# Eight x tiles in flight, LoRA loads in one place, first mixing blocks issued by ScalarE, and weighted factors rounded ahead of the second layer's rows

## The reference, cut to what matters

```python
# layer 0: per sequence, rows mixed by a 64x64 matrix
y = einsum('bct,bcd->bdt', x, L0_cond_weights[itok_B_0_15])
h = relu(layernorm(y @ gw1.T + gb1) * gamma + beta)        # 32 hidden units
gates = h @ gw2.T + gb2                                    # 8 experts, the best 2, softmax
w = factors of the two experts, 0 where an expert has over 768 tokens
x1 = x + y @ weight.T + einsum((y @ lora_A) * w, lora_B) / 16   # 8 experts x rank 16
# layer 1: per sequence one of 8 weights of 1024x1024
z = einsum('bsi,boi->bso', x1, L1_cond_weight[itok_B_3_7])
gate, up = bitlinear(z, w_gate), bitlinear(z, w_up)        # weights rounded to -1, 0, 1 by mean |w|
out = x1 + bitlinear(gate * up, w_down)
```

## Time and profile before

| | us |
|---|---|
| median of 3 executions | 1399.43 |
| lowest, highest | 1396.98, 1400.17 |
| the profiled execution's own time | 1401.02 |
| its span, first to last instruction | 1399.3 |
| TensorE busy | 1330.5 (95% of the span) |
| VectorE, ScalarE, GpSimd busy | 726.4, 391.1, 157.4 |
| mean granted TensorE clock | 0.985 |

### The profile page before, as it was taken

The page is one execution under the profiler, slowest core; times in us unless marked ns, Lnnn a source line. Parts: engine busy times, 40 slices in busy tenths (PEclk is TensorE's granted clock), DMA queues, the critical chain, the costliest instruction groups (busy, mean ns, idle before and its releaser), DMA issues.

```text
span 1399.3 us, 24300 instructions
## 1 busy us (share of the span) xinstructions
PE 1330.5 (95%) x8864; PEld 850.5 (61%) x8865; DVE 726.4 (52%) x1143; ACT 391.1 (28%) x437; POOL 157.4 (11%) x114
## 2 busy tenths in 40 slices
PE   6787699999999998999999999999999999999998
PEld 5773344444454444555544788854788844888843
DVE  5375455411255565888865355573355582455521
ACT  3464343200111135888730011120011110111100
POOL 5100000000101000000000023320133310222310
PEclk9998899999999999999999999999999999999999
DMA  9976699967996926999964643353634455544354
GB/s 235 231 255 212 249 401 416 346 166 149 284 264 227 272 98 241 354 361 350 315 251 159 237 150 136 143 216 128 222 150 157 147 188 186 205 157 153 128 196 143
DMA packets 174626, 310.70 MB, mean 222 GB/s; under 512 B 99392, under 2 KB 131520, under 8 KB 166752
## 3 DMA queue, kind: packets, MB, share of 16 engines
q1 hardware_dynamic: 156048, 242.77, 53.6%
q10 hardware_dynamic: 14032, 43.97, 8.8%
q0 software_dynamic: 4480, 23.07, 4.6%
HBM read 220.78 MB, written 68.03 MB: 206 GB/s over the span
## 4 chain that ended last, share of the span: by engine, by line
PE 79%; DMA 8%; DVE 4%; issue 3%; ACT 2%; SPq 2%; POOL 1%; ACTq 0%; DVEq 0%; POOLq 0%
PE pair L969 27%; PE pair L1006 15%; PE pair L841 12%; PE pair L933 10%; PE pair L757 9%; DMA region_w<-in_L_ffn_w_gate 2%; DMA region_q<-wb_scratch 2%; PE pair L668 2%; PE pair L887 2%; DMA w1s_scratch<-region_q 1%; PE pair L764 1%; ACT region_w L1088 1%; POOL region_w L653 1%; SPq L448 1%; ACT region_q L1039 1%
## 5 line engine op out<-in xcount | busy, mean ns | idle before, releaser
L969 PE MATMUL pair<-act_t,region_q 128*128 128x256 f16 x3696 | 404.0, 273 | 0.0
L969 PEld LDWEIGHTS pair<-act_t,region_q 128*128 128x128 f16 x3696 | 361.6, 98 | 42.5
L1006 PE MATMUL pair<-region_q,region_w 128*128 128x512 f16 x1232 | 267.6, 379 | 4.7 <-DMA region_q<-wb_scratch 4.4
L1006 PEld LDWEIGHTS pair<-region_q,region_w 128*128 128x128 f16 x1232 | 120.1, 98 | 150.9 <-DMA region_q<-wb_scratch 5.9
L653 POOL TENSOR_TENSOR region_w<-region_q,region_w 128x1792 f32 (+1 forms) x33 | 118.4, 3588 | 732.4 <-ACT region_w L1244 732.4
L841 PE MATMUL pair<-region_w,act_t 128*128 x816 | 180.2, 381 | 2.0 <-DVE region_q L1571 2.0
L757 PE MATMUL pair<-region_w,act_t 128*128 128x512 f16 x768 | 172.5, 382 | 0.0
L933 PE MATMUL pair<-act_t,region_q 128*128 128x512 f16 x704 | 157.9, 383 | 1.4 <-issue 1.4
L841 PEld LDWEIGHTS pair<-region_w,act_t 128*128 x816 | 80.2, 98 | 95.8 <-issue 4.3
L1250 ACT ACTIVATE region_q<-pair 128x512 f32<-128x512 f32 x33 | 19.7, 597 | 403.7 <-PE pair L969 403.7
L757 PEld LDWEIGHTS pair<-region_w,act_t 128*128 (+1 forms) x768 | 75.6, 99 | 88.2 <-issue 2.5
(11 more groups left out here) (184 smaller groups left out, 1016.4 us busy)
## 6 DMA issues: line engine op xcount, KB each, us to landing
region_q<-wa_scratch SPq DMA_DIRECT2D x33, 1792.0 KB, 7.3
region_q<-wb_scratch SPq DMA_DIRECT2D x28, 1408.0 KB, 5.9
region_q<-in_L_cond_weight SPq DMA_DIRECT2D x40, 512.0 KB, 9.4
w1s_scratch<-region_q ACTq DMA_DIRECT2D x40, 512.0 KB, 7.9
wa_scratch<-region_q SPq DMA_DIRECT2D x22, 896.0 KB, 6.2
region_q<-in_x SPq DMA_DIRECT2D x64, 256.0 KB, 6.5
region_w<-in_L_ffn_w_gate ACTq DMA_DIRECT2D x17, 640.0 KB, 5.4
wb_scratch<-region_q SPq DMA_DIRECT2D x11, 896.0 KB, 4.1
```

Source lines behind the costliest of these rows:

```text
L969: mm = pe.matmul(bank(s_bank, b)[:, (1 - h) * HALF:(2 - h) * HALF], ring_a[s][:, h, o_a, k], moving[a], start=(opens and h == 1 and k == 0 ...
L1006: mm = pe.matmul(bank(s_bank, b), iop[:, a, p, o_a, tp * P:(tp + 1) * P], ring_b[r][:, p], start=(opens and p == 0 and a == 0), stop=(not ...
```

## The change

- x goes through eight buffers (`NMIX`), a tile at a time, SP reading eight fields of the order at once; the buffer of tile t is free when tile t-8 is mixed. All LoRA-A loads stand ahead of tile 8, LoRA B behind tile 15.
- The mixing blocks of tiles 0 and 1 are issued by ScalarE, before its first rounding; GpSimd starts with tile 2.
- Gate products start after the mix of tile 9; LoRA A is rounded after tile 8; w_gate loads start at tile 10; square roots are taken at tiles 12 and 14, and that of the third quarter behind the loop, where its moments are now taken too. In the moments the mean's scaling and the subtraction are one instruction.
- Blocks 4 to 7 of the first adapter are rounded and stored behind the weighted factors, between the first x1 parts, on ScalarE and on VectorE.
- SP loads tiles 2 and 3 of x together and then the eight row blocks of the second adapter.
- The second layer's first product waits for 15 residuals.

```diff
@@ -71,8 +71,10 @@
 SUMS = {11: (0,), 12: (1, 2), 13: (3, 4), 14: (5, 6), 15: (7, 8)}
-GATES = {11: (0, 1), 12: (2, 3, 4), 13: (5, 6, 7), 14: (8, 9, 10, 11), 15: (12, 13, 14, 15)}
-LORA_AFTER = {2: (1,), 4: (2, 3), 6: (4, 5), 8: (6, 7)}
+GATES = {9: (0, 1), 10: (2, 3), 11: (4, 5), 12: (6, 7), 13: (8, 9, 10), 14: (11, 12), 15: (13, 14, 15)}
+NMIX = 8
+SQRTS = {12: 0, 14: 1}
+LORA_AT = 8
 NPIECE = 24
@@ -129,7 +131,7 @@
         x1_nat = [view(region_q, 40 + 4 * i, [D], F32) for i in range(2)]
-        mix_nat = [x_nat[0], x_nat[1], view(region_q, 48, [D], F32), view(region_q, 52, [D], F32)]
+        mix_nat = [view(region_q, kb, [D], F32) for kb in (32, 36, 48, 52, 16, 20, 24, 28)]
         gw1_nat = x1_nat[0]
@@ -441,12 +444,11 @@
             def load_mix(t, perm):
-                for s in range(2):
-                    wait_if(sp, y_done, t + s - 3)
-                    slot = (t + s) % 4
-                    for h in range(2):
-                        sp.dma_start(mix_nat[slot][h * SEQ:(h + 1) * SEQ, :], x_rows[ds(perm[2 * s + h] * SEQ, SEQ), :])\
-                          .then_inc(mix_loaded[slot], 16)
+                slot = t % NMIX
+                wait_if(sp, y_done, t - NMIX + 1)
+                for h in range(2):
+                    sp.dma_start(mix_nat[slot][h * SEQ:(h + 1) * SEQ, :], x_rows[ds(perm[h] * SEQ, SEQ), :])\
+                      .then_inc(mix_loaded[slot], 16)
@@ -455,17 +457,18 @@
                 load_w(w0[r * P:(r + 1) * P, :], r, r)
-            load_lora(0)
             sp.wait_ge(index_ready, 1)
-            for t in range(0, NT, 2):
-                load_mix(t, fields(sp, F_PERM + 2 * t, 4, NB - 1))
-                if t < 4:
-                    for r in range(4 + t, 6 + t):
-                        load_w(w0[r * P:(r + 1) * P, :], r, r % 4)
-                for k in LORA_AFTER.get(t, ()):
-                    load_lora(k)
-                if t == 10:
-                    sp.dma_start(lora_b_nat, lora_b.rearrange("e r o -> (e r) o")).then_inc(lora_b_loaded, 16)
+            for t0 in range(0, NT, 4):
+                perm = fields(sp, F_PERM + 2 * t0, 8, NB - 1)
+                for t in range(t0, t0 + 4):
+                    if t == LORA_AT:
+                        for k in range(KC):
+                            load_lora(k)
+                    load_mix(t, perm[2 * (t - t0):2 * (t - t0) + 2])
+                    if t in (1, 4):
+                        for r in range(4, 6) if t == 1 else range(6, 8):
+                            load_w(w0[r * P:(r + 1) * P, :], r, r % 4)
+            sp.dma_start(lora_b_nat, lora_b.rearrange("e r o -> (e r) o")).then_inc(lora_b_loaded, 16)
             sp.wait_ge(index_ready, INDEX_ALL)
@@ -497,7 +500,16 @@
-            with sp.Fori(1, 6) as i:
+            for t in range(2, 4):
+                sp.wait_ge(acc_released, t - 1)
+                load_pair(x_nat[t - 2], x_loaded[t - 2], t)
+            used = field(sp, F_USED, 0, NADP)
+            row_1 = field(sp, F_ADP, 1, NADP - 1) * D
+            with sp.If(used > 1):
+                for t in range(2, 4):
+                    for q in range(4):
+                        load_w(w1_rows[ds(row_1 + (4 * t - 8 + q) * P, P), :], NPREP0 + 4 * t + q, q)
+            with sp.Fori(2, 6) as i:
                 layer0(i)
@@ -611,7 +623,7 @@
                 for s in range(2):
-                    wait_if(pool, cond_loaded[c + s], 32 * i)
+                    wait_if(pool, cond_loaded[c + s], 32 * i if c > 0 else 0)
                     for h in range(2):
@@ -619,7 +631,7 @@
             for i in range(2):
-                for c in range(0, 8, 2):
+                for c in range(2 - 2 * i, 8, 2):
                     load_cond(i, c)
@@ -711,7 +723,7 @@
                 pe.wait_ge(mix_loaded[slot], loads)
-                pe.wait_ge(cond_loaded[t % 8], 32 * (t // 8 + 1))
+                pe.wait_ge(cond_first[t] if t < 2 else cond_loaded[t % 8], 32 * (t // 8 + 1 if t % 8 > 1 else 1))
                 wait_if(pe, y_low, t - 1)
@@ -735,7 +747,7 @@
                     pe.wait_ge(index_ready, INDEX_ALL)
-                mix(t, t % 4, (t + 1) % 2, 32 * (t // 4 + 1))
+                mix(t, t % NMIX, (t + 1) % 2, 32 * (t // NMIX + 1))
                 if t == 0:
@@ -829,7 +841,7 @@
                     pe.wait_ge(x1_low, 2)
-                    pe.wait_ge(acc_released, NT)
+                    pe.wait_ge(acc_released, NT - 1)
                 pe.wait_ge(w1_loaded, rank * 16 + 16)
@@ -1044,6 +1056,13 @@
+            act.wait_ge(index_ready, 1)
+            act.wait_ge(consts_ready, 8)
+            cond = fields(act, F_COND, 4, 15)
+            for t in range(2):
+                for h in range(2):
+                    act.dma_start(cond_bd[h * SEQ:(h + 1) * SEQ, t, h * SEQ:(h + 1) * SEQ],
+                                  cond_rows[ds(cond[2 * t + h] * SEQ, SEQ), :]).then_inc(cond_first[t], 16)
             high_w0(0)
@@ -1094,8 +1113,6 @@
                     tmp_part(n)
-                if t == 13:
-                    gate_sqrt(0)
                 y_part(t, (t + 1) % 2)
@@ -1104,20 +1121,22 @@
                     act.dma_start(small[t - 2][0], small[t - 2][1].partition_broadcast(P)).then_inc(small_loaded, 16)
-                if t in (9, 10):
-                    load_gate(t - 9)
                 if t == 10:
+                    for p in range(2):
+                        load_gate(p)
+                if t == 8:
                     act.wait_ge(lora_loaded, 16 * KC)
...
                         .then_inc(ag_high, 1)
-                if t >= 14:
-                    gate_sqrt(t - 13)
+                if t in SQRTS:
+                    gate_sqrt(SQRTS[t])
                 for p in SUMS.get(t, ()):
...
             high(lb[:, 0, :], lora_b_nat, WGT_SCALE).then_inc(ag_high, 1)
+            gate_sqrt(2)
@@ -1132,16 +1151,12 @@
                 store_w(o, o)
-                rank0_part(o + 4)
-                sum_gate(13 + o)
-            sum_gate(17)
-            for o in range(4, 7):
-                store_w(o, o - 4)
+            for p in range(13, 17):
+                sum_gate(p)
             for i in range(2):
...
                 high(tmpw_t[:, 0, i * D:(i + 1) * D], pair[2][:, :], 1.0).then_inc(tmpw_high, 1)
-                if i == 0:
-                    store_w(7, 3)
+            sum_gate(17)
@@ -1157,8 +1172,16 @@
+            rank0_part(4)
+            rank0_part(5)
+            store_w(4, 0)
             x1_part(0, 0)
+            rank0_part(6)
+            store_w(5, 1)
             x1_part(1, 1)
+            rank0_part(7)
+            store_w(6, 2)
+            store_w(7, 3)
             with act.Fori(1, NT // 2) as i:
@@ -1467,8 +1490,8 @@
                 gthen(v.tensor_reduce(tot, hq, X, ALU.add))
-                gthen(v.tensor_scalar(tot, tot, 1.0 / GH, None, ALU.mult))
-                gthen(v.tensor_tensor(hq, hq, per_tile(tot, GH), ALU.subtract))
+                gthen(v.scalar_tensor_tensor(out=hq, in0=per_tile(tot, GH), scalar=-1.0 / GH, in1=hq,
+                                             op0=ALU.mult, op1=ALU.add))
                 gthen(v.tensor_tensor(sq, hq, hq, ALU.mult))
@@ -1500,19 +1523,20 @@
                     low_w0(t + 3)
-                if t == 10:
+                if t == 8:
                     v.wait_ge(ag_high, 2)
...
                         ag[:, 0, :, 0:ER]).then_inc(ag_low, 1)
-                if t == 12:
+                if t == 11:
                     v.wait_ge(small_loaded, 80)
                     gate_moments(0)
+                elif t == 12:
                     gate_logits(0)
...
                     gate_logits(1)
-                    gate_moments(2)
+            gate_moments(2)
             gate_logits(2)
@@ -1556,8 +1580,6 @@
             ins.then_inc(tmpw_ready, 1)
-            for o in range(4, KC):
-                low_w(o, o - 4)
             for i in range(2):
@@ -1584,9 +1606,13 @@
             residual(1, 1, pair[1])
+            low_w(4, 0)
+            low_w(5, 1)
             low_x1(0)
             residual(2, 0, pair[3])
+            low_w(6, 2)
             low_x1(1)
+            low_w(7, 3)
             prep_low(1, 2)
```

More of the change, by code:

```diff
@@ L230, in build_program @@
         w_loaded = [sem(f"w_loaded{i}") for i in range(4)]
-        mix_loaded = [sem(f"mix_loaded{i}") for i in range(4)]
+        mix_loaded = [sem(f"mix_loaded{i}") for i in range(NMIX)]
         cond_loaded = [sem(f"cond_loaded{i}") for i in range(8)]
+        cond_first = [sem(f"cond_first{i}") for i in range(2)]
         x_loaded = [sem(f"x_loaded{i}") for i in range(2)]
```

## The result

| | before | after |
|---|---|---|
| median (lowest to highest, executions) | 1399.18 (1396.98 to 1401.44, 8) | 1393.07 (1387.89 to 1396.11, 8) |
| ratio, 95% interval | | 0.9953 [0.9935, 0.9971] |
| profiled execution, its span | 1401.02, 1399.3 | 1387.89, 1386.2 |

The change makes the kernel 6.1 us faster, where 21 were forecast; 1393 lies outside the range of 1367 to 1391. The profiled execution is the fastest of the eight. It won 8.7 us up to the second layer's first product (330.1 to 321.4); the other 4.4 of its 13.1 lie behind that product, where the changed stages play no part: from there to the end it took 1064.8 us, and 1069.2 before. As far as the runs show this is chance: in the 18 profiles of this document that rest ranges from 1064.8 to 1069.5 us, and in a second one of the changed kernel (after_again) it was 1068.9.

The account below looks back on a forecast made before the run. It took TensorE's waits before 177.5 us, then a DMA-bound adapter stage, as the bound; 5.5 (opening) + 13.4 (adapter stage) + 2.0 (last residual) = 20.9 off gave 1378 us, 8 in 10 within 1367 to 1391.

Parts of the forecast that it names:

- the larger term (stores behind the factors): First adapter's rounds and stores behind the factors: next adapter stage starts earlier, worth 13.4 us (8 to 17).
- the opening: Eight tiles, LoRA loads together, first blocks by ScalarE: start of first main product (E) 5.5 us earlier (0 to 9).
- 42 to 50, I take 46: Opening: tile 8 of x arrives at 46 us, first gate product near 52, first main product (E) at 92.
- The late root: Gate chain: third quarter's root behind copies and LoRA B's round ends the factors' multiply about 4 us later; 1 shows.
- Rival A: Opening gives nothing, as eight tiles share saturated DMA engines and E stays; 1384 us, chance 0.15.
- Its wait of 17.9 becomes 1.0 + 3.8 = 4.8: TensorE's wait for the rounded factors, once stores no longer precede them: 4.8 us (2 to 10).
- Rival D: Factors stay blocked: gate pieces 15 and 16 take 12.31 us, factors 6 us later; 1384 us, chance 0.12.
- 3.9 us behind the residual: with the change E+47.7: Next adapter's first row load follows the second residual by 3.9 us, at E+47.7 instead of E+63.1: 15.4 earlier.
- So this is a DMA chain: First row load to TensorE's turn of tile 10, 107.3 us, is DMA-bound; 15.4 earlier less 2 for stores gives 13.4.
- my test of 113 us: Forecast is wrong if first row load to TensorE's turn of tile 10 takes over 113 us.
- The last residual, 2.0: Second layer's first product no longer waits for the last tile's residual: 2.0 us earlier (0 to 2.0).
- Rival B: Adapter stage gets dearer as loads, stores and blocks 4 to 7 mix; 1443 us at 260 GB/s, chance 0.07.

Follow-up runs that it names:

- lora_flat: Changed kernel with LoRA A's bytes read by one load of 128 long rows instead of eight loads of small packets; 1388.94 us.
- late_root: Kernel before with only the third quarter's square root moved behind the last gate copies and LoRA B's round; 1403.89 us, ratio 1.0024.
- opening_root_early: Kernel before with only the opening part, third quarter's root ahead of the last gate copies, gate sums 8 and 9 later; 1401.23 us, ratio 1.0006.
- sums_behind: Changed kernel with gate sums 15 and 16 behind the factors' rounds and 17 behind the last store; 1384.39 us.
- rows_as_before: Changed kernel with SP's old order of x tiles 2 and 3 and the next adapter's row blocks; 1393.61 us.
- three: Changed kernel with the square root early, the gate sums behind the factors and the old row order together; 1381.67 us, ratio 0.9870.
- half_rows: Changed kernel with row loads of the second to fifth adapters cut to 512 of 1024 columns; 1391.25 us.
- factors_only: Kernel before with only the rounds and stores of weight blocks 4 to 7 moved behind the weighted factors; 1393.37 us.
- three_flat: Changed kernel with root early, sums behind, old row order, and LoRA A's bytes in 128 large packets; 1375.42 us.
- all_residuals: Changed kernel with the second layer's first product waiting for all 16 residuals again; 1394.42 us.

## Why the prediction was wrong, step by step

The direction was right, and so was the place of the larger term (stores behind the factors); the opening, forecast at 5.5 us, gave nothing. Five steps failed, and 1, 2 and 4 are one error: I priced an order on one engine by its instructions and not by what they wait for.

1. **x8 at "42 to 50, I take 46", E = 92.** Failed by 3 us. I had seen the eight LoRA loads ahead of x8 but not that their issues hold SyncE 15.13 us; what was won there was won with fewer packets (lora_flat: E = 90.1), so I read the 0.99 busy DMA engines at 225 GB/s in the earlier trace rows as busy with small ones. The clock fell too: 1.2 GHz from 45.7 to 52.5 us, from within the wait of 6.74 on. From the first gate product to E it took 38.6 us, for 37.9 and 2 more for the sums; the first mix came 2.3 us earlier, for 2.5, though kernels with the old code there had a first mix from 15.0 to 16.9, so part of the 2.3 is chance.

2. **The late root: "then ends at about E+29.7", "1 us of it shows".** The multiply ended at E+30.7 in the changed kernel, and its delay shows at the factors' turn as E+30.8 for E+28.6, 2.2 us where I had 1. In profiles with a longer stand of the sum ahead of it it was E+32.8 to E+36.5. I had counted 0.9 and 1.0 for copies and round, but ScalarE's queue ahead of the root also holds a sum that waits for a gate piece. Together 1 and 2 are Rival A's result by another way: E moves by 2.5, and the factors' turn by 0.3 (126.1 to 125.8). late_root and opening_root_early show that this order costs time, and that with the root early the opening is no loss.

3. **"Its wait of 17.9 becomes 1.0 + 3.8 = 4.8".** It became 6.95, for 3.8 (the 1.0 stood at the factors' turn): the mechanism is right, the term mis-sized. Piece 15 was asked for at E+27.3 and not E+26, and took 8.8 us for 6, between the median of 5.1 and the 12.31 of the earlier trace rows, which is Rival D in part; the first rounded half of the factors was ready at E+41.4 for E+37. The wait could have been nothing (sums_behind), as no one needs these sums before the second layer.

4. **"3.9 us behind the residual: with the change E+47.7".** The largest failure: E+58.9. Of these 11.2 us 4.5 are the step itself: the 3.9 was read off a kernel in which SyncE asks only for tile 2's pair before the rows, and the diff puts tile 3's pair and its fields there too (8.4 us from the residual's end); rows_as_before takes these 4.5 away without a gain. The other 6.7 are the residual's own: it ended at 145.45, E+50.5, for E+43.8. Of them 4.4 come from item 3, and 2.4 lie between the two halves of the factors: I had 4.4 us from one low round to the next, and it took 6.8 (135.13 to 141.96), as it had before:

```profile
146.36 1.22 DVE L1344 SCALAR_TENSOR_TENSOR region_q<-pair,region_q 128x1024 f16<-128x1024 f32 x1 [1.33 <-ACT region_q L1039]
...
153.18 1.23 DVE L1344 SCALAR_TENSOR_TENSOR region_q<-pair,region_q 128x1024 f16<-128x1024 f32 x1 [5.60 <-ACT region_q L1039]
```

Both profiles show 1.2 GHz there (134.4 to 141.3 after). In `three`, at 2.4 GHz, it took 4.8 us.

5. **"So this is a DMA chain": 15.4 - 2 = 13.4.** The 107.3 us from first row to the turn of tile 10 came out at 107.5 (153.89 to 261.4), and my test of 113 us passed, but for another reason than I gave: half_rows takes a sixth of the bytes away without a gain. So the first row's time does not set the stage: in rows_as_before it came 2.7 us earlier and the turn of tile 10 was no earlier (113.9 us behind it). What sets it, I read, is order. From VectorE's start on residuals 0 and 1 to the turn of tile 3 it took 23.0 to 23.2 us in all four profiled kernels with the stores ahead of the factors, and 27.3 to 29.4 in all others. Between the two now stand the rounds of blocks 4 to 7: the adapter's row blocks go into the buffers of these blocks (`load_w` waits for `w_low` of the block that was in its buffer), and VectorE rounds blocks 6 and 7 at 153.91 and 156.17 only, behind a residual of tile 2 that by the profile waits 3.48 us for a store of x1. The residual of tile 3 (170.64) is behind the rows' rounds. Thus 11.2 us won at the residuals (154.3 to 143.1) were 5.6 at tile 3 (177.5 to 171.9). I had put the price of the moved stores at 2 us of DMA; the lag grew by 4 to 6 us. This reading of the cause is from the queue order and the profiles; that the lag splits by the place of the stores in all 18 profiles is what is shown, and that it is 27.4 us in half_rows too, so that bytes are 1.5 of it at most. No run leaves the four rounds out or moves them on their own.

In `three`, with rows 22.7 us earlier, the stage took 113.2 us, but so it did with the old row order elsewhere (112.2 in factors_only, 113.9 in rows_as_before); from the turn of tile 3 to that of tile 10 it took 91.0, for 90.5 before and 89.5 after. That TensorE is the bound there is said by its row after: 89.48 busy of 89.50. TensorE waited 0.45 and 0.30 us at the turns of tiles 9 and 10 in `three`; three_flat, with rows 5.3 us earlier again, still gained 6.3, so the transfers are no bound there yet.

6. **The last residual, 2.0.** Right: the wait went, and came back with all_residuals.

The sum as it came out, by profile: E 2.5, taken by the root (0.3 left at the factors' turn); at the LoRA products 11.2; at tile 3 5.6; at the turn of tile 10 6.6, where 18.9 were forecast; at the second layer 8.7, of which 2.0 is the last residual. Of the 12.3 us missing at tile 10, 3.0 are E, 6.7 the residual and 5.7 the lag from there to tile 3 (28.8 for 23.1), less 3.0 by which the rest did better than forecast (1.0 from tile 3 on, and the 2 counted for the moved stores). The medians say 6.1 where the two profiles say 8.7: the profiled execution of before is 1.8 us above its median and that of after 5.2 below, so the last microseconds can't be told from chance. Rival B (a dearer mixture) did not come: 409 GB/s. The Trainium skill's 358 GB/s ("DMA: Bandwidth & Descriptors", "Where 436 GB/s comes from") is passed in the changed kernel too, by 409 over 105 us.

## What to carry to other kernels

Before a step is moved on an engine, write down what every instruction ahead of it in that queue waits for, and price it by the longest of those waits: a root of 0.2 us behind a sum that waits for DMA left VectorE idle for 3.4 to 5.7 us, and a load behind one more tile's loads and fields 4.6. When work is moved behind a stall, ask whose buffer it held: here half of the 11.2 us was gone again one tile later, by my reading through four rounds that the next loads wait for. And where DMA engines are busy at half of their rate, count packets before bytes or order.

## What the hardware showed that I had not expected

- Eight issues of 1024 packets of 64 B held the issuing engine 15.13 us behind one another, and 0.59 to 0.60 each when spread; one issue of the same bytes in long rows took 0.34.
- The granted clock fell to 1.2 GHz for 3.4 to 6.8 us after short stands of TensorE at the count product: after those of 2.17, 2.22, 3.50, 5.35 and 5.68 us a stretch of half clock began at 118 to 121 us; after those of 0.56, 0.76, 1.20 and 1.86 none did, and none where there was no such wait. It does not go by the wait alone: a wait of 2.48 us for tile 8 in three_flat was followed by none. In the LoRA wait of 6.95 (129.5 to 136.4) one of 6.9 us began, at 134.4; six LoRA matmuls took 2.74 us in it, and 1.46 at 159.89. A wait there can thus cost more than its own length; no run shows what these stretches cost the kernel.
